# Attention's seven banks shared by maxima and scores by a fixed table, with double reads of maxima and a reordered front

## The chip, the cores and the metric

The kernel runs on one core of one Trainium2 chip. Measured is the device time of one execution in microseconds; before the change it is 4558.4 us (median of three, 4558.05 to 4560.63). PE is TensorE, ACT is ScalarE, DVE is VectorE, POOL is GpSimd, SP is SyncE.

## What is computed

Two transformer layers over 4096 tokens of width 256. Each layer adds an attention and a feed-forward branch, both read from the same normalised x.

```python
x = L0_attn_x                                   # (1, 4096, 256)
xn = _layernorm(x)
x = x + _L0_attn_ref(xn, ...) + _L0_ffn_ref(xn, ...)   # block-local linear attention; fp6-quantised linear
xn = _layernorm(x)
x = x + _L1_attn_ref(xn, ...) + _L1_ffn_ref(xn, ...)   # 16-head softmax attention; shared + 8 experts, top 2
# inside _L1_attn_ref: a layer norm of its own, q, k with rotary tables, head width 16
scores = jnp.einsum('bhqd,bhkd->bhqk', q, k)
attn = jax.nn.softmax(scores, axis=-1)
out = jnp.einsum('bhqk,bhkd->bhqd', attn, v)
```

## The kernel before, in words

The program has four phases, each with a program for every engine, ordered by semaphores alone: `front` (layer 0 and the inputs of layer 1), `attention` (layer 1's softmax attention, and on POOL the scatter of rows to the experts), `routed_experts`, and a tail.

**front** goes over 8 blocks of 512 tokens in 11 rounds. Four stages run in a round, each on another block: p (normalise, transpose, project to q, k, v; quantise), a (features of the linear attention, its windows, sums and division, the quantised linear), b (the two layer norms of layer 1, their transposes, the gate) and d (layer 1's q, k, v, the rotation, the split into three bf16 parts). PSUM holds four banks F for features, two banks W for the windows, sums and the output of a, and two banks G for all transposes and projections of p, b and d. On PE a round is: features 0 and projections d, features 1 and projections d, features 2 and values d, features 3, transposes of XD and XN (`turned`, L569, both into G), windows (L588), p's projections (L617, L623), sums (L603), transposes of XN1 and Z, the gate (L693), the outputs (L703, L708). DVE makes the products QP (L467), `turn` (L511, L512), the masks (L473), the moments, `quantise` (L416 to L428) and `divide` (L480, L481). POOL adds or subtracts for the rotation (L298), computes reciprocal roots, adds the bias to X2 (L319) and computes the lower bf16 parts (L326, L329).

**attention** has 4 groups of 4 heads and 8 blocks of 512 queries, 32 blocks n in all. A block has 128 chunks c, one for each of 32 key tiles u and 4 heads. For a chunk PE computes scores^T (128 keys x 512 queries, L1022), ACT takes the exponential into a ring of 12 (L1103), and PE weights the values with it (`weigh`, L1036: four heads side by side, columns of 32). The softmax's shift must be known before: for the block after next and the next one, PE computes 64 pairs of maxima products (`max_pair`, L1010: two heads side by side, 64 rows each), and DVE reduces each product of 512 to its maximum (L1185). At the end of a block's pairs DVE reduces them to 16 shifts (L1213), POOL splits these in two bf16 (L889 to L891), PE transposes them (L1016), DVE copies them out (L1200) and SP stores them as rows of QS (L965), so that the score products subtract them. Each block ends on ACT with a copy of the result (L1114), and ACT's program is a loop over blocks.

PE's order for round u, written out by hand: pair 2u, weighting of u-1, pair 2u+1, four scores of u+1. That is four changes of the kind of tile (64 rows, 32 columns, 64 rows, full). PSUM: four banks ST for scores, taken in turn; three banks MP for maxima, taken in turn; one bank OT for the result. A maxima product waits until its bank's last reduction is done (`room`: `mp_free`, counted per reduction). Before the first block there is a head: 64 pairs of block 0, its shifts, 12 pairs (`LEAD`) of block 1.

At the start of attention DVE computes the routing of tokens to experts in a chain of small steps (L1126 to L1178), among them the slots of the rows (L1173), after which POOL scatters. POOL first sets constant rows of KS and QS with eight memsets (L903, L904). SP issues the loads of two groups (L933, L940, L946) and only behind them the first store of shifts (L965).

Of the kernel before, what the change touches and what calls it, by code (L numbers as in the profile page):

```python
# [103 lines left out]
def front(nc, io, scr, LG):  # L104


    with ExitStack() as ctx:
        def sb(name, shape, dt=f32):
# [6 lines left out]
                 "wq_ready bias_ok store_t store_p store_v store_r store_x store_z spare")  # L115
# [150 lines left out]
        def _(pool):  # L266
# [26 lines left out]
            for it in range(ROUNDS):  # L293
                p, a, b, d = blocks(it)
                if d is not None:
                    for m in range(4):
                        pool.wait_ge(S["c_drain"], d * NC + m // 2 * 2 + 2)
                        G_.tensor_tensor(rc[:, m, :], rc[:, m, :], rs[:, m, :],  # L298
                                         ALU.add if m % 2 else ALU.subtract).then_inc(S["rot_ready"], 1)
# [13 lines left out]
                if a is not None:  # L313
                    if it == 1:
                        pool.wait_ge(S["w_load"], 16 * LOADS_W)
                        G_.tensor_tensor(bias0[:, 0, :], bias0[:, 0, :], bias0[:, 1, :], ALU.add).then_inc(S["bias_ok"], 1)
                        pool.wait_ge(S["bias_ok"], 1)
                    pool.wait_ge(S["x2_load"], 16 * (a + 1))
                    G_.tensor_tensor(X2[:], X2[:], bias0[:, 0, :].unsqueeze(1).to_broadcast([P, TPB, D]),  # L319
                                     ALU.add).then_inc(S["xb_ready"], 1)  # L320
                if d is not None:
# [5 lines left out]
                    for m in range(4):  # L327
                        pool.wait_ge(S["mid_ready"], d * 4 + m + 1)
                        G_.tensor_tensor(parts[:, 2, m, :], rc[:, m, :], parts[:, 1, m, :], ALU.subtract).then_inc(S["lo_ready"], 1)  # L329
                if p is not None and p + 1 < NB:  # L330
                    incoming(p + 1)

        @block.scalar
        def _(act):
# [10 lines left out]
            for it in range(ROUNDS):  # L345
                p, a, b, d = blocks(it)
                if a is not None:
                    for g in range(4):
                        features(a, g)
                    for k in range(DC):  # L350
                        act.wait_ge(S["x_fill"], a * NX + k + 1)
                        A.copy(xdT[:, k, :], G[:, k, :]).then_inc(S["x_drain"], 1)
                if p is not None:
                    for k in range(DC):
                        act.wait_ge(S["p_fill"], p * NP_ + k + 1)
                        A.copy(xnT[:, k, :], G[:, k, :]).then_inc(S["p_drain"], 1)
                if d is not None:
                    at_least(act, S["store_p"], d * 96)
                    for m in range(4):
                        act.wait_ge(S["rot_ready"], d * 4 + m + 1)  # L360
                        A.copy(parts[:, 0, m, :], rc[:, m, :]).then_inc(S["hi_ready"], 1)
                if b is not None:
# [8 lines left out]
                if p is not None:  # L371
                    for m in range(2 * DC):
                        act.wait_ge(S["p_fill"], p * NP_ + DC + m + 1)
                        A.copy(qkT[:, m, :], G[:, m % 2, :]).then_inc(S["p_drain"], 1)
                    for u in range(2):
                        act.wait_ge(S["p_fill"], p * NP_ + 3 * DC + u + 1)
                        A.copy(v0[:, p % 2, 2 * u:2 * u + 2, :].rearrange("p t c -> p (t c)"),
                               G[:, u, :]).then_inc(S["p_drain"], 1)
# [6 lines left out]
                if d is not None:  # L385
                    for m in range(4):
                        act.wait_ge(S["r1_ready"], d * 4 + m + 1)
                        A.copy(parts[:, 1, m, :], rc[:, m, :]).then_inc(S["mid_ready"], 1)
                if b is not None:
# [6 lines left out]
                    for k in range(DC):  # L396
# [9 lines left out]
        def _(dve):  # L406
# [96 lines left out]
            def turn(d, m):  # L503
                dve.wait_ge(S["c_fill"], d * NC + m + 1)
                if m == 0:
# [5 lines left out]
                V.scalar_tensor_tensor(to[:, 2 * n, :], bank, bqk[:, m:m + 1], tab[:, odd, :], ALU.add, ALU.mult)  # L511
# [13 lines left out]
            for it in range(ROUNDS):  # L525
# [7 lines left out]
                for g in range(4):  # L533
# [3 lines left out]
                    if d is not None and g < 2:  # L537
                        turn(d, 2 * g)
                        turn(d, 2 * g + 1)
                    if d is not None and g == 2:  # L540
                        values(d, 0)
                        values(d, 1)
                if b is not None:
                    outgoing_moments(b)
                if a is not None:
                    for h in range(H0):
                        mask(a, h)
                if p is not None:
# [15 lines left out]
        def _(pe):  # L564
# [7 lines left out]
            def features(a, g):  # L572
# [9 lines left out]
                last.then_inc(S["f_fill"], 4)  # L582

# [45 lines left out]
            for it in range(ROUNDS):  # L629
# [13 lines left out]
                if a is not None:  # L643
                    features(a, 1)
                if d is not None:
# [10 lines left out]
                if a is not None:  # L656
                    features(a, 3)
                    pe.wait_ge(S["xd_ready"], a + 1)
                    turned(free, XD, "x_fill")
                    free = ("x_drain", a * NX)  # L660
                if p is not None:
                    pe.wait_ge(S["xn_ready"], (p + 1) * TPB)
                    turned(free, XN, "p_fill")
                if a is not None:
# [1061 lines left out]
```

## Time and profile before

| | us |
|---|---|
| median of the runs | 4558.4 |
| profiled execution, its own time | 4568.3 |
| its span | 4566.5 |

Busy over the span: PE 92%, DVE 73%, ACT 58%, POOL 9%. The clock granted to PE is 0.96 of full speed in the mean, 0.87 in the front, 0.50 in the head of attention and 1.00 in its blocks. The groups of instructions name the costliest: DVE's 4096 reductions of maxima (686 ns each), ACT's 4096 exponentials (605 ns), PE's weightings, scores and maxima. Two engines are busy for over nine tenths in attention, so how long a round takes, and who waits in it, has to be read from the order of single instructions (the timeline). In a timeline row the first number is the start, the second the time until the last instruction of the row ends; x2 is the number of instructions; idle time before them stands in brackets.

### The profile page before, as it was taken

The page shows a single profiled execution, that of the slowest core. Times are in us where ns is not written, and L with a number is a line of the kernel's source. Part 1 is how long each engine was busy: PE and PEld are TensorE (multiplying, and loading weights), DVE is VectorE, ACT ScalarE, POOL GpSimd, SP SyncE. Part 2 cuts the span into 40 slices and gives each one's busy share as a digit, 9 for nine tenths or more (in the row PEclk, how much of TensorE's full clock was granted, in tenths as well). Part 3 has the DMA queues.
Part 4 walks back from the last instruction along what each step waited for, and adds up shares of the span by engine and source line. Part 5 has one row for each costly group of instructions (what it writes and reads, how often), then busy time and mean ns, then how long its engine had stood idle before and what let it go on. Part 6 is the DMA issues. An engine that isn't in the chain of part 4 may idle for free. (4 is left out here: it accounts for less than half of the span.)

```text
span 4566.5 us, 69687 instructions
## 1 busy us (share of the span) xinstructions
PE 4187.5 (92%) x23454; PEld 1823.3 (40%) x23748; DVE 3338.7 (73%) x5188; ACT 2661.5 (58%) x5113; POOL 426.7 (9%) x476
## 2 busy tenths in 40 slices
PE   6888715999999999999999999999998899999999
PEld 3665501222222222222222222222224788886666
DVE  6878578999999999999999999999980011132332
ACT  4445301777777777777777777777786222222222
POOL 0333465000000000000000000000000100011110
PEclk8989856999999999999999999999999999999999
DMA  4232384000002200002200000000003855532221
GB/s 145 75 97 74 106 146 138 4 4 6 4 4 33 50 4 6 4 4 34 50 4 6 4 4 6 4 4 6 4 6 103 248 193 193 193 122 58 63 69 42
DMA packets 206159, 264.59 MB, mean 58 GB/s; under 512 B 24881, under 2 KB 169521, under 8 KB 204241
## 3 DMA queue, kind: packets, MB, share of 16 engines
q1 hardware_dynamic: 193872, 228.98, 17.3%
q0 software_dynamic: 11904, 31.10, 2.4%
q8 instruction: 169, 2.77, 0.3%
q14 instruction: 214, 1.75, 0.1%
HBM read 184.76 MB, written 74.97 MB: 57 GB/s over the span
## 5 line engine op out<-in xcount | busy, mean ns | idle before, releaser
L1185 DVE TENSOR_REDUCE a_MX<-a_MP 128x1 f32<-128x512 f32 x4096 | 2635.9, 686 | 108.8 <-PE a_MP L1010 64.8
L1103 ACT ACTIVATE a_PT<-a_ST 128x512 f32<-128x512 f32 x4096 | 2108.0, 605 | 770.7 <-PE a_ST L1022 462.4
L1036 PE MATMUL a_OT<-a_PT,a_VG 128*32 128x512 f32 x8192 | 1092.8, 605 | 0.8 <-ACT a_PT L1103 0.5
L1022 PE MATMUL a_ST<-a_QS,a_KS 128*128 128x512 bf16 x3802 | 1036.2, 383 | 59.7 <-ACT a_PT L1103 24.5
L1010 PE MATMUL a_MP<-a_KS,a_QS 64*128 64x512 bf16 x4096 | 816.3, 395 | 129.6 <-DVE a_MX L1185 67.2
L1010 PEld LDWEIGHTS a_MP<-a_KS,a_QS 64*128 64x128 bf16 x4096 | 197.0, 93 | 1399.1 <-DVE a_MX L1185 1324.5
L1022 PEld LDWEIGHTS a_ST<-a_QS,a_KS 128*128 128x128 bf16 x4096 | 319.6, 98 | 554.4 <-ACT a_PT L1103 305.9
L1371 ACT ACTIVATE e_hT<-e_up,e_BF 128x256 f32<-128x256 f32 x312 | 147.9, 474 | 414.8 <-PE e_up L1324 414.7
L1324 PE MATMUL e_up<-e_xT,e_WF 128*128 128x256 f32 x1248 | 324.7, 383 | 0.8 <-DVE e_xT L1381 0.8
L1333 PE MATMUL e_dn<-e_WP,e_hT 128*128 128x256 f32 x1248 | 321.9, 381 | 0.0
L1381 DVE COPY e_xT<-e_tp 128x512 f32<-128x512 f32 x39 | 27.0, 692 | 364.8 <-PE e_tp L1317 364.8
L1036 PEld LDWEIGHTS a_OT<-a_PT,a_VG 128*32 128x32 f32 x8192 | 161.2, 108 | 235.4 <-ACT a_PT L1103 217.1
L1333 PEld LDWEIGHTS e_dn<-e_WP,e_hT 128*128 128x128 f32 x1248 | 238.1, 191 | 33.3
L1324 PEld LDWEIGHTS e_up<-e_xT,e_WF 128*128 128x128 f32 x1248 | 237.2, 193 | 32.5 <-DVE e_xT L1381 1.2
L889 POOL CAST a_negparts<-a_neg 128x16 bf16<-128x16 f32 x31 | 6.1, 196 | 2597.7 <-DVE a_neg L1213 2597.7
L1388 DVE TENSOR_TENSOR e_Y<-e_dn,e_BP 128x256 f32<-128x256 f32 x78 | 32.0, 424 | 233.7 <-PE e_dn L1333 233.5
L1634 ACT ACTIVATE u_hT<-u_a,t_bfs 128x512 f32<-128x512 f32 x64 | 44.0, 687 | 194.4 <-PE u_a L1589 163.2
L342 ACT ACTIVATE f_E<-f_F 128x512 f32<-128x512 f32 x128 | 79.8, 623 | 128.1 <-PE f_F L581 128.1
L1634 ACT ACTIVATE u_hT<-u_a,t_b1c 128x512 f32<-128x512 f32 x64 | 44.0, 687 | 176.4 <-PE u_a L1589 176.4
L1471 DVE RECIPROCAL t_DEN<-t_DEN 128x512 f32<-128x512 f32 x16 | 53.6, 3348 | 116.6 <-DMA t_xT<-scr_xn1T 116.6
L467 DVE SCALAR_TENSOR_TENSOR f_QP<-f_E,f_R 128x512 f32<-128x512 f32 x128 | 102.1, 826 | 37.4 <-ACT f_R L343 36.8
L1599 PE MATMUL u_d<-t_wps,u_hT 128*128 128x256 f32 x512 | 120.9, 379 | 0.0
(219 smaller groups left out, 2810.0 us busy)
## 6 DMA issues: line engine op xcount, KB each, us to landing
e_WF<-Wfc SPq DMA_DIRECT2D x39, 1024.0 KB, 5.0
e_WP<-Wproj SPq DMA_DIRECT2D x39, 1024.0 KB, 7.1
a_QS<-scr_qparts SPq DMA_DIRECT2D x384, 32.0 KB, 7.3
a_KS<-scr_kparts SPq DMA_DIRECT2D x48, 256.0 KB, 12.5
scr_xs<-f_zero SPq DMA_DIRECT2D x1, 9984.0 KB, 33.0
e_XS<-scr_xs SPq DMA_DIRECT2D x39, 256.0 KB, 2.7
scr_ys<-e_Y SPq DMA_DIRECT2D x39, 256.0 KB, 2.1
f_X<-x SPq DMA_DIRECT2D x16, 512.0 KB, 4.7
```

The lines of the kernel that those rows point to most:

```text
L342: A.activation(E[:, u % ER, :], F[:, j, :], ACT.Exp)
L467: V.scalar_tensor_tensor(QP[:, g // 2 * 4 + j, g % 2, :], E[:, u % ER, :], 1.0, R[:, u % ER, :], ALU.min, ALU.add).then_inc(S["feat"], 1)
L1010: T.matmul(bank(e + side), QS[j][half, bass.ds((b * HG + hs) * BLK + t * P, P)], KS[j][half, hs, kb * BLK:(kb + 1) * BLK], start=True, sto ...
L1022: T.matmul(ST[:, c % SBANKS, :], KS[j][:, h, u * P:(u + 1) * P], QS[j][:, bass.ds((b * HG + h) * BLK, BLK)], start=True, stop=True).then_i ...
L1036: last = T.matmul(OT[w, :], VG[j][:, u, w], PT[:, (HG * u + h) % RING, :], start=u == 0, stop=u == KT - 1)
L1103: nc.scalar.activation(PT[:, c % RING, :], ST[:, c % SBANKS, :], ACT.Exp, scale=SOFT_SCALE).then_inc(S["exp_done"], 1)
L1185: last = V.reduce_max(MX[n % 2][:, side, x:x + 1], bank(e + side), AX.X).then_inc(S["mp_free"], 1)
L1324: last = T.matmul(UP[:, m % UPB, 0:ET], WF[j][:, k, m * P:(m + 1) * P], xT[j][:, k, :], start=k == 0, stop=k == DC - 1)
L1333: last = T.matmul(DN[:, t, 0:D], hT[j][:, m, t * P:(t + 1) * P], WP[j][:, m, :], start=m == 0, stop=m == HC - 1)
L1371: nc.scalar.activation(hT[j][:, m, :], UP[:, m % UPB, 0:ET], ACT.Gelu_apprx_tanh, bias=BF[j][:, m:m + 1]).then_inc(S["hid_ready"], 1)
L1599: last = T.matmul(DN[:, t // 2, t % 2 * D:(t % 2 + 1) * D], hT[:, u % HR, t * P:(t + 1) * P], down_w[half][:, m, :], start=u == 0 and t % ...
L1634: nc.scalar.activation(hT[:, u % HR, :], A[:, use % BANKS, :], ACT.Relu if u >= HC else ACT.Gelu_apprx_tanh, bias=(tt["b1c"] if u >= HC el ...
```

## The change

In attention, the banks ST and MP become one tensor PS of seven. Which bank a chunk or a pair takes is fixed by a table with a period of eight chunks and four pairs, that is two rounds. PE's order for such a period: weighting, pairs 0 and 1, three scores, weighting, pair 2, five scores, pair 3. It has seven changes of the kind of tile. Pairs 1 and 3 are reduced by one instruction over two neighbouring banks, pairs 0 and 2 by two as before; `mp_free` now counts up by two for a double read. Waits on `ends[i]` are for the last reduction of pair i of the period. The head takes three pairs of banks in turn, all read two at once. PE's head waits for the slots, and POOL's memsets wait for them too.

In the front, XD and XN are transposed into the banks W, XD behind features 0 and XN behind features 1, and ACT's copies of them follow the same places. The rotation's additions go from POOL to DVE (`rotate`). DVE makes the masks before the moments of b. ACT copies q, k and v of p before the norms of b, and copies xn1T before the middle parts, which alternate with zT. POOL adds the bias to X2 behind the parts and after the quantising.

```diff
-SBANKS, MBANKS = 4, 3
+ABANKS = 7
+
+MAX_BANKS = ((4, 5), (0, 1), (2, 5), (2, 3))
+SCORE_BANKS = (2, 3, 6, 3, 4, 1, 0, 6)
+HEAD_BANKS = ((0, 1), (2, 3), (4, 5))
+HEAD_TURN, TURN = 6, 4
+PERIOD = len(SCORE_BANKS)
...
+        def score_bank(c):
+            return PS[:, SCORE_BANKS[(c - HG) % PERIOD], :]
...
+                event = [first_event(n)]
+
+                def pair(x):
+                    if x < PAIRS - LEAD and next1:
+                        max_pair(MAX_BANKS[x % 4], *next1, x + LEAD)
+                    elif x >= PAIRS - LEAD and next2:
+                        max_pair(MAX_BANKS[x % 4], *next2, x - PAIRS + LEAD)
+                    else:
+                        return
+                    event[0] += SIDES
+                    ends[x % 4] = event[0]
...
+                for k in range(KT // 2):
+                    c = PERIOD * k + HG
+                    at = n * CHUNKS + c
+                    if k:
+                        weigh(n, 2 * k - 1)
+                    elif n:
+                        weigh(n - 1, KT - 1)
+
+                    pe.wait_ge(S["exp_done"], at - 3)
+                    pe.wait_ge(S["mp_free"], ends[2])
+                    pair(4 * k)
+
+                    pe.wait_ge(S["exp_done"], at - 1)
+                    pair(4 * k + 1)
+
+                    pe.wait_ge(S["mp_free"], ends[3])
+                    issue(c)
+                    issue(c + 1)
+                    pe.wait_ge(S["exp_done"], at)
+                    issue(c + 2)
+                    weigh(n, 2 * k)
+
+                    pe.wait_ge(S["mp_free"], ends[0])
+                    turned = 2 * k + 1 == TURN_MAX and next1
+                    if turned:
+                        negmax_transpose(TURN, n + 1)
+                        event[0] += 1
+                        turned = event[0]
+                    pe.wait_ge(S["exp_done"], at + 1)
+                    pair(4 * k + 2)
+
+                    pe.wait_ge(S["exp_done"], at + 2)
+                    issue(c + 3)
+                    if turned:
+                        pe.wait_ge(S["mp_free"], turned)
+                    if c + HG == CHUNKS and next1:
+                        pe.wait_ge(S["negmax_load"], 16 * SIDES * (n + 2))
+                    issue(c + 4)
+
+                    pe.wait_ge(S["mp_free"], ends[1])
+                    issue(c + 5)
+                    issue(c + 6)
+                    pe.wait_ge(S["exp_done"], at + 3)
+                    issue(c + 7)
+
+                    if c + 3 < CHUNKS:
+                        pe.wait_ge(S["exp_done"], at + 4)
+                    pe.wait_ge(S["mp_free"], ends[2])
+                    pair(4 * k + 3)
...
+            def two_maxima(n, e, banks, x):
+
+                dve.wait_ge(S["mp_full"], e + SIDES)
+                V.tensor_reduce(MX[n % 2][:, :, x], PS[:, banks[0]:banks[0] + SIDES, :], AX.X,
+                                ALU.max).then_inc(S["mp_free"], SIDES)
...
+                    take = two_maxima if x % 2 else maximum
...
             pool.wait_ge(S["ident_ok"], 1)
+            pool.wait_ge(S["slots_ok"], TOPK)
             for j in range(2):
                 for side in range(SIDES):
...
+            def rotate(d, n):
+
+                dve.wait_ge(S["turned"], d * 4 + 2 * n + 2)
+                dve.wait_ge(S["c_drain"], d * NC + 2 * n + 2)
+                for m in (2 * n, 2 * n + 1):
+                    V.tensor_tensor(rc[:, m, :], rc[:, m, :], rs[:, m, :],
+                                    ALU.add if m % 2 else ALU.subtract).then_inc(S["rot_ready"], 1)
...
+                w_free = ("w_drain", b * NW + W_OUT) if b is not None else None
                 if a is not None:
                     features(a, 0)
+                    pe.wait_ge(S["xd_ready"], a + 1)
+                    turned_w(w_free, XD, "x_fill")
+                    w_free = ("x_drain", a * NX)
...
+                if p is not None:
+                    pe.wait_ge(S["xn_ready"], (p + 1) * TPB)
+                    turned_w(w_free, XN, "p_fill")
+                    w_free = ("p_drain", p * NP_)
```

## Rows read from the trace of the kernel before

**Rows 1.** Attention's full blocks: us, busy PE, PEld, DVE, ACT, POOL, PEclk, DMA, GB/s.

```profile
759.00:3422.00 2663.00, 2582.12 (x15599) 658.29 (x15885) 2549.41 (x4008) 2062.30 (x4003) 37.06 (x113) 1.00 0.06 12
```

**Rows 2.** Timeline of PE, one round: start us, us, engine line op names shapes xcount.

```profile
2055.68 0.39 PE L1010 MATMUL a_MP<-a_KS,a_QS 64*128 64x512 bf16 x2
2056.00 1.06 PE L1036 MATMUL a_OT<-a_PT,a_VG 128*32 128x512 f32 x8
2056.99 0.39 PE L1010 MATMUL a_MP<-a_KS,a_QS 64*128 64x512 bf16 x2
2057.32 1.04 PE L1022 MATMUL a_ST<-a_QS,a_KS 128*128 128x512 bf16 x3
2058.29 0.39 PE L1010 MATMUL a_MP<-a_KS,a_QS 64*128 64x512 bf16 x2
```

**Rows 3.** Timeline: DVE's reads beside PE's pairs.

```profile
2002.68 1.38 DVE L1185 TENSOR_REDUCE a_MX<-a_MP 128x1 f32<-128x512 f32 x2
2004.26 0.39 PE L1010 MATMUL a_MP<-a_KS,a_QS 64*128 64x512 bf16 x2
...
2062.29 0.39 PE L1010 MATMUL a_MP<-a_KS,a_QS 64*128 64x512 bf16 x2
2062.72 0.69 DVE L1185 TENSOR_REDUCE a_MX<-a_MP 128x1 f32<-128x512 f32 x1 [1.40 <-PE a_MP L1010]
```

**Rows 4.** Timeline of the head, where PE waits for DVE.

```profile
745.08 1.29 DVE L1185 TENSOR_REDUCE a_MX<-a_MP 128x1 f32<-128x512 f32 x2
745.82 0.10 PEld L1010 LDWEIGHTS a_MP<-a_KS,a_QS 64*128 64x128 bf16 x2 [1.29 <-issue]
```

**Rows 5.** The reduction to shifts, once a block: durations, first and last start.

```profile
L1213 DVE TENSOR_REDUCE a_neg<-a_MX x31: 286/287/289, 841.0 to 3409.1; 128x16 f32<-128x128 f32 x31
```

**Rows 6.** Timeline at a block's edge, and ACT in the last block.

```profile
2039.94 0.29 DVE L1213 TENSOR_REDUCE a_neg<-a_MX 128x16 f32<-128x128 f32 x1
...
2049.02 0.20 DVE L1200 COPY a_negT<-a_MP 32x128 bf16<-32x128 bf16 x1
...
2057.21 0.58 ACT L1114 COPY a_OS<-a_OT 128x512 f32<-128x512 f32 x1
2059.85 3.04 ACT L1103 ACTIVATE a_PT<-a_ST 128x512 f32<-128x512 f32 x6 [2.06 <-PE a_OT L1036]
...
3422.45 61.03 ACT L1103 ACTIVATE a_PT<-a_ST 128x512 f32<-128x512 f32 x124
```

**Rows 7.** DVE's reduction of 1024 elements in quantising: durations ns min/median/max, first and last start.

```profile
L416 DVE TENSOR_REDUCE f_sc<-f_XN x8: 1207/1207/1221, 9.5 to 440.6; 128x32 f32<-128x1024 f32 x8
```

**Rows 8.** Timeline before attention's first score.

```profile
603.49 6.77 DVE L1152 COPY a_PT<-a_PT 128x16 f32<-128x16 f32 x1
...
644.93 0.17 DVE L1158 TENSOR_SCALAR a_PT<-a_PT 128x8 f32<-128x8 f32 x1
...
652.76 1.29 DVE L1185 TENSOR_REDUCE a_MX<-a_MP 128x1 f32<-128x512 f32 x2 [0.82 <-PE a_MP L1010]
...
709.05 0.43 SPq L946 DMA_DIRECT2D a_VG<-scr_va  x1
...
758.88 0.13 PEld L1022 LDWEIGHTS a_ST<-a_QS,a_KS 128*128 128x128 bf16 x2 [0.44 <-issue]
```

**Rows 9.** Timeline of one round of the front, and POOL in its last.

```profile
338.94 3.40 PE L708 MATMUL f_W<-f_wout,f_attT 128*128 128x256 f32 x15
...
362.49 1.16 PE L569 MATMUL f_G<-f_ident,f_XD 128*128 128x128 f32 x8 [1.77 <-DVE f_va L519]
365.44 1.94 PE L569 MATMUL f_G<-f_ident,f_XN 128*128 128x128 f32 x8 [1.78 <-ACT f_xdT L352]
...
393.61 1.06 PE L569 MATMUL f_G<-f_ident,f_Z 128*128 128x128 f32 x8 [3.14 <-ACT f_xn1T L393]
...
403.11 3.62 PE L708 MATMUL f_W<-f_wout,f_attT 128*128 128x256 f32 x16
...
569.40 2.50 POOL L298 TENSOR_TENSOR f_rc<-f_rc,f_rs 128x512 f32<-128x512 f32 x2 [0.99 <-DVE f_rs L512]
```

More of the change, by code:

```diff
@@ L346, in _ @@
                 p, a, b, d = blocks(it)
-                if a is not None:
-                    for g in range(4):
+                for g in range(4):
+                    if a is not None:
                         features(a, g)
[L350 to L356, printed above, removed]
+                    if a is not None and g == 0:
+                        for k in range(DC):
+                            act.wait_ge(S["x_fill"], a * NX + k + 1)
+                            A.copy(xdT[:, k, :], W[:, k, :]).then_inc(S["x_drain"], 1)
+                    if p is not None and g == 1:
+                        for k in range(DC):
+                            act.wait_ge(S["p_fill"], p * NP_ + k + 1)
+                            A.copy(xnT[:, k, :], W[:, k, :]).then_inc(S["p_drain"], 1)
                 if d is not None:
@@ L361, in _ @@
                         A.copy(parts[:, 0, m, :], rc[:, m, :]).then_inc(S["hi_ready"], 1)
+                if p is not None:
+                    for m in range(2 * DC):
+                        act.wait_ge(S["p_fill"], p * NP_ + DC + m + 1)
+                        A.copy(qkT[:, m, :], G[:, m % 2, :]).then_inc(S["p_drain"], 1)
+                    for u in range(2):
+                        act.wait_ge(S["p_fill"], p * NP_ + 3 * DC + u + 1)
+                        A.copy(v0[:, p % 2, 2 * u:2 * u + 2, :].rearrange("p t c -> p (t c)"),
+                               G[:, u, :]).then_inc(S["p_drain"], 1)
                 if b is not None:
@@ L395, in _ @@
                         act.wait_ge(S["w_load"], 16 * LOADS_W)
-                    for k in range(DC):
+                for m in range(4):
+                    if d is not None:
+                        act.wait_ge(S["r1_ready"], d * 4 + m + 1)
+                        A.copy(parts[:, 1, m, :], rc[:, m, :]).then_inc(S["mid_ready"], 1)
+                    if b is not None and m % 2:
+                        k = m // 2
                         act.wait_ge(S["b_fill"], b * NB_ + DC + k + 1)
@@ L582, in features, with turned_w @@
                 last.then_inc(S["f_fill"], 4)
+            def turned_w(free, src, fill):
+                for k in range(DC):
+                    if free:
+                        at_least(pe, S[free[0]], free[1] + k + 1)
+                    transposes(W[:, k, :], src, k).then_inc(S[fill], 1)
             def windows(a, h):
@@ L657, in _ @@
                     features(a, 3)
[L658 to L664, printed above, removed]
+                    pe.wait_ge(S[w_free[0]], w_free[1] + DC)
                     for h in range(H0):
@@ L998, in _, with max_pair @@
             T = nc.tensor
-            def room(e):
-                pe.wait_ge(S["mp_free"], e + 1)
-            def max_pair(e, j, b, x):
+            ends = [HEAD_EVENTS] * len(MAX_BANKS)
+            def max_pair(banks, j, b, x):
                 h, t, kb = x // (TPB * KB), x // KB % TPB, x % KB
-                room(e + SIDES - 1)
                 for side in range(SIDES):
                     hs, half = side * HS + h, slice(side * HALF, (side + 1) * HALF)
-                    T.matmul(bank(e + side), QS[j][half, bass.ds((b * HG + hs) * BLK + t * P, P)],
+                    T.matmul(PS[:, banks[side], :], QS[j][half, bass.ds((b * HG + hs) * BLK + t * P, P)],
@@ L1011, in max_pair @@
                              KS[j][half, hs, kb * BLK:(kb + 1) * BLK], start=True, stop=True).then_inc(S["mp_full"], 1)
-            def negmax_transpose(e, n):
-                room(e)
-                wait_alone(pe, S["negmax_ready"], n + 1, S["spare"])
-                T.transpose(negT_ps(e), negparts[:].rearrange("p s r c -> p (s r c)"), identb[:]).then_inc(S["mp_full"], 1)
-            def scores(n, j, b, u):
-                for c in range(HG * u, HG * (u + 1)):
-                    pe.wait_ge(S["exp_done"], n * CHUNKS + c + 1)
-                    h = c % HG
-                    T.matmul(ST[:, c % SBANKS, :], KS[j][:, h, u * P:(u + 1) * P],
-                             QS[j][:, bass.ds((b * HG + h) * BLK, BLK)], start=True, stop=True).then_inc(S["qk_done"], 1)
@@ L1029, in weigh, with score @@
+            def score(n, j, b, c):
+                h, u = c % HG, c // HG
+                T.matmul(score_bank(c), KS[j][:, h, u * P:(u + 1) * P],
+                         QS[j][:, bass.ds((b * HG + h) * BLK, BLK)], start=True, stop=True).then_inc(S["qk_done"], 1)
             def weigh(n, u):
                 j = n // NB % 2
-                pe.wait_ge(S["exp_done"], n * CHUNKS + HG * (u + 1) + SBANKS)
+                pe.wait_ge(S["exp_done"], n * CHUNKS + HG * (u + 1))
                 if u == 0:
@@ L1075, in _ @@
             for x in range(LEAD):
-                max_pair(SIDES * (PAIRS + x) + 1, 0, 1, x)
-            scores_first(0, 0, 0)
+                head_pair(PAIRS + x, SIDES * (PAIRS + x) + 1, 0, 1, x)
+            pe.wait_ge(S["mp_free"], HEAD_EVENTS)
+            pe.wait_ge(S["negmax_load"], 16 * SIDES)
+            for c in range(HG):
+                score(0, 0, 0, c)
             for G in range(NG):
@@ L1114, in one_block @@
                 nc.scalar.copy(OS[:], OT[:]).then_inc(S["o_copied"], 1)
-            for c in range(SBANKS):
+            for c in range(HG):
                 exp(0, c)
```

156 lines of the change are left out of this document (62 added, 94 removed).

## The prediction

> **What bounds the kernel now.** I read the busy time by stretch first: the front ends at 588, attention's first scores come at 759, its full blocks end at 3422 and the last block at 3486; the experts and the tail behind it aren't touched. In the full blocks PE is busy for 2582 of 2663 us (97%) and VectorE for 2549 (96%) [rows 1], so the groups of instructions can't say which of them sets the pace. The timeline can [rows 2]. One round of PE starts a maxima pair at 2055.68, the weighting at 2056.00, a pair at 2056.99, four scores at 2057.32 and the next pair at 2058.29: 0.32 + 0.99 + 0.33 + 0.97 = 2.61 us, the same in round after round. A score takes 0.22 and a pair alone the same; what is over, about 0.10, comes at each of the four changes of tile kind. VectorE's two reads of a pair together span 1.29, one alone 0.69 [rows 3], so the second begins 0.61 after the first: four reads need 2.43 of the 2.61. Nor does PE wait for them: in the head, where it does, its weights start 0.05 after a read ends (745.08 + 0.69 = 745.77, then 745.82) [rows 4], but in the round the read of 2002.68 + 0.69 = 2003.37 to 2004.06 is followed by a pair only at 2004.26 [rows 3]. **PE's order of work is the bound**, VectorE comes 7% behind it.
>
> A block lasts (3409.1 - 841.0)/30 = 85.60 us [rows 5]; 32 rounds are 83.5, and 2.1 are left: VectorE idles for 1.40 behind ScalarE's block loop (copy at 2057.21, next exponential only at 2059.85), and the transposition of the maxima with its copy and the wait for it make the rest [rows 3, 6].
>
> **Attention, the steady round.** Two rounds are now one period: weighting, pairs P0 and P1, three scores, weighting, P2, five scores, P3. There are seven changes for eight, all on PE, so by PE alone the period is 2 x 2.61 - 0.10 = **5.12 us** for 5.22. P1 and P3 are read two banks at once. No row shows that read from PSUM; the nearest is the 1024-element reduction in SBUF, 1207 ns beside the 0.69 of a PSUM read of 512 [rows 3, 7]: 512 more elements for 0.52. So I take 1.21, with the next read 1.13 after its start. VectorE then needs 4 x 0.61 + 2 x 1.13 = 4.70 of 5.12, which looks like room.
>
> The bank table takes it away. P3 is issued only when mp_free has reached ends[2], that is when both reads of P2 are done, and VectorE reads in order P0 (two single reads), P1 (one double), P2 (two single). From P0's start: 0.43 until the first read (2062.29 to 2062.72) [rows 3], 0.61, 0.61, then the double for 1.13, then 0.61 and 0.68 to the end of P2: 4.07. Release 0.05, so P3 starts at 4.12. Where would PE be? P0 and P1 0.22 + 0.32, three scores 0.66 + 0.10, weighting 0.99, P2 0.32, five scores 1.08 + 0.10: 3.79. It waits 0.33. After P3 come 0.32 and a weighting of 1.00 before the next P0, and VectorE has nothing to read in that time but P3: free again at 0.43 + 1.13 = 1.56 behind P3's start, while P0's products are there at 1.32 + 0.43 = 1.75. The cycle closes over both engines: 4.12 + 1.32 = **5.44 us per two rounds, 0.22 more than now**. The other new waits hold: P1's read frees its banks at 0.43 + 1.22 + 1.21 + 0.05 = 2.91 for a score (the third behind P2) due at about 3.05; P3's frees its own 0.15 before the first score of the next period; and the exponential of the score behind P2, for which P3 waits too, is done at 2.62 + 0.5 + 0.6 = 3.7, 0.4 ahead of P3 (a product ends 0.39 after its start [rows 2], six exponentials take 3.04, some 0.6 for one and 0.48 from one to the next [rows 6]). Ends for the unknown double: it would have to cost 0.33 less than 1.13 for PE to be the bound again; that is 0.80 for 1024 elements, and the SBUF row excludes it unless PSUM reads two banks faster than one. A cost above is possible: 0.1 more would be 1.6 us a block.
>
> The rule against which I weighed the gain is in the Trainium skill, "TensorEngine Tiling (Array Packing)", Key Properties: changing the tiling mode drains TensorE. The trace agrees: the 0.10 at each change. By that rule alone the period would be 5.12.
>
> **The block's edge.** ScalarE's copy and loop jump (2.64 from the copy's start to the exponential [rows 6], for 0.5 without them) delay the first exponential of the next block's second score group by 1.8 against the schedule; P2 needs its bank, so P2 moves by 1.2 and P3 by 1.1 (now 1.4). The copy of the transposed maxima (0.20 plus its own wait) stands in VectorE's queue before P2, which is in the cycle: 0.3. The small reduction before P0 (0.29 [rows 6]) takes the reads some 0.2 later, and there is room for 0.05: 0.15. Together 1.5 for 2.1. A block: 16 x 5.44 + 1.5 = 88.6, **+3.0; 31 blocks: +93 us**. With 0.05 of doubt in the cycle this is 70 to 120.
>
> **The last block** has no pairs and is bound by exponentials: 61.0 us for 124 [rows 6]. The new order makes a score wait for a weighting twice in eight (0.2 and 0.35 late): 16 x 0.45 = **+7 us** (0 to 12).
>
> **The head.** Before, GpSimd's eight memsets (6.9 each) run beside VectorE's routing steps, and from 603.49 on each small copy or scalar step there lasts until a memset ends: 41 us until 644.93 for ten instructions that take some 2.3 undisturbed [rows 8]. The memsets now wait for the slots, so these 39 us go. The slots are ready at about 611; the first loads have been issued from 588.6 on at 0.5 each and land, at 12.5 us for one of the keys' (the page), at about the same time. The moved memsets can hold the last two small steps instead (up to 2 x 6.9), so the maxima begin at 612 to 626; I take 625. 64 pairs take 64 x 1.13 = 72 (now 76 pairs and the shifts fill 652.76 to 758.88, 1.4 a pair [rows 8]), then 2, then 12 x 1.13: 713. But SyncE stores the negated maxima only behind both groups' loads, whose last is issued at 709.05 [rows 8] and, as the page has it, needs 10.2 us: the first score comes at about 720 for 758.88: **-38 us** (-30 to -48). GpSimd's scatter starts some 16 later and ends by 806 for 790; the first block's shifts are wanted at about 805, so it just hides.
>
> The shared port behind this is also in the Trainium skill, "SBUF - State Buffer", SBUF: two separate sides: VectorE in a two-port mode and GpSimd lock each other out for a whole instruction. The trace agrees, 6.8 us each.
>
> **The front.** A round lasts 64.2 us (the weighting by w_out at 338.94 and 403.11). In it PE idles 1.77 before the XD transposes, 1.78 before XN, and 3.14 before Z [rows 9], and 2.8 in three smaller gaps. The transposes move into banks W between features, so the first two gaps go, but the masks wait for the last features on ScalarE, which stay: windows end some 3 earlier. Splitting ScalarE's copies (xn1T ahead of the middle parts) takes 2 of the 3.14, while XN1 and Z behind the value copies give back 1. The rotation leaves GpSimd for four VectorE steps of about 0.65 (a VectorE step of 512 elements, [rows 3], is the nearest row); VectorE's products beside it ran slower by as much, so that is even. I get 3.7 a round for seven rounds and 3.4 at the end, where the rotation on GpSimd stands in the last chain (2.50 for two of its four steps [rows 9]): **-30 us** (-10 to -50). The moved bias addition waits for X2, reloaded 12 later; it ends about 2 before it is needed. If that cover goes, 2 us a round go too.
>
> **Sum.** -30 - 38 + 93 + 7 = +32 on the profile's 4568.3 us (span 4566.5), so 4600 there; the median of the runs is 4558.4, 9.9 lower, so **4590 us**.
>
> **Rivals.** (1) PE sets the period after all: if VectorE's chain from P0 to P2's end is under 3.74, P3 doesn't wait. That is 5.12, 5.1 us a block less than in my sum: 4590 - 159 = 4431. For it speaks the total of 4.70 for VectorE, against it the chain above. 0.10. (2) The steady loss is right, but front and head give all they can (-50, -48) and the cycle is 5.40: -20 - 10 - 20 = 4540. 0.08. (3) The loads, the scatter or the bias addition eat half of the gain in front and head: 4590 + 34 = 4624; together with a double read of 1.2 spacing 4660. 0.14. The forecast itself has 0.68, with a range of 4560 to 4620.
>
> 0.2% is 9 us, about what a measurement of this kernel can tell from no change. Under 4549: (1), most of (2): 0.16. Within: 0.06. Above: 0.78. The range takes in (2) and half of (3): 4540 to 4640.
>
> **What the profile will show.** Pairs P3 of successive periods 5.44 apart, PE's weights of P3 idle behind VectorE by some 0.3, none elsewhere; double reads of 1.21; 88.6 between two small reductions; first score near 720; front's end near 558. Wrong would be: a double read far from 1.21, a change from scores straight to the weighting that costs much more than 0.10 and over the slack of 0.33, or GpSimd's scatter late for the first block.

## The result and the profile after

The changed kernel takes 4626.5 us (median of four runs, 4624.3 to 4627.5) where the kernel before takes 4559.2 beside it: 1.0147 times as long, 95% interval 1.0129 to 1.0164. Forecast were 4590, slower, within 4540 to 4640. The sign and the waiting pair held; the loss is 67 us where the sum gave 32. The profiled execution of after took 4626.0 (span 4624.2), 57.7 more than the one of before, so the two profiles show 58 of the 67 us; the other 9 are the size of a stall that the profile of before has in its first block (before_again, below).

The page of after, its busy times and the costliest groups. A read of two banks takes 1221 ns, one of a single bank 684:

```profile
PE 4179.7 (90%) x23748; PEld 1784.1 (39%) x23748; DVE 3141.6 (68%) x4158; ACT 2666.9 (58%) x5113; POOL 374.8 (8%) x444
...
L1253 DVE TENSOR_REDUCE a_MX<-a_PS 128x2 f32<-128x1024 f32 x1062 | 1290.4, 1221 | 326.6 <-PE a_PS L1031 326.5
L1259 DVE TENSOR_REDUCE a_MX<-a_PS 128x1 f32<-128x512 f32 x1972 | 1266.3, 684 | 48.7 <-PE a_PS L1031 42.2
...
L1031 PE MATMUL a_PS<-a_KS,a_QS 64*128 64x512 bf16 x4096 | 730.7, 391 | 261.0 <-ACT a_PT L1172 160.3
```

VectorE has lost 197 us of work (3338.7 before) and the kernel is slower: VectorE's load was not what set the pace. PE idles 261 us ahead of the maxima pairs, where it idled 130. Busy time by stage of after (front; head; blocks; last block), in the columns of [rows 1]. The blocks have PE at 2573 of 2781 us, where it was at 2582 of 2663 [rows 1]:

```profile
0.00:553.00 553.00, 442.61 (x2948) 313.23 (x2948) 394.86 (x627) 265.94 (x515) 135.69 (x155) 0.90 0.33 108
553.00:679.00 126.00, 48.09 (x159) 9.26 (x160) 116.77 (x138) 0.42 (x1) 74.67 (x33) 0.50 0.93 165
679.00:3460.00 2781.00, 2572.76 (x15812) 625.95 (x15811) 2402.56 (x3019) 2058.61 (x3978) 68.76 (x144) 1.00 0.06 13
3460.00:3543.00 83.00, 73.86 (x445) 17.44 (x443) 0.21 (x1) 76.57 (x149) 0.58 (x3) 1.00 0.01 4
```

The reduction to shifts, once a block, the counterpart of [rows 5]. The 30 blocks between the first and the last take (3459.6 - 752.9)/30 = 90.2 us each, for 85.6:

```profile
L1289 DVE TENSOR_REDUCE a_neg<-a_MX x31: 285/286/288, 752.9 to 3459.6; 128x16 f32<-128x128 f32 x31
```

Stage by stage, in us from the timelines (first attention load, first score, first and last such reduction, last score, end of the span):

| | front | to the first score | to the first reduction | 30 blocks | to the last score | rest |
|---|---|---|---|---|---|---|
| before | 587.7 | 171.2 | 82.1 | 2568.1 | 72.5 | 1084.9 |
| after | 553.0 | 125.6 | 74.3 | 2706.7 | 82.8 | 1081.8 |
| difference | -34.7 | -45.6 | -7.8 | +138.6 | +10.3 | -3.1 |

One period of after, of all engines. Read it by P0 (2002.78), P2 (2005.06) and P3 (2006.96):

```profile
2002.78 0.61 PE L1031 MATMUL a_PS<-a_KS,a_QS 64*128 64x512 bf16 x4
2003.20 1.29 DVE L1259 TENSOR_REDUCE a_MX<-a_PS 128x1 f32<-128x512 f32 x2
...
2004.41 1.22 DVE L1253 TENSOR_REDUCE a_MX<-a_PS 128x2 f32<-128x1024 f32 x1
2005.06 0.39 PE L1031 MATMUL a_PS<-a_KS,a_QS 64*128 64x512 bf16 x2
2005.38 1.25 PE L1046 MATMUL a_PS<-a_QS,a_KS 128*128 128x512 bf16 x5
2005.54 1.28 DVE L1259 TENSOR_REDUCE a_MX<-a_PS 128x1 f32<-128x512 f32 x2
2006.93 0.12 PEld L1031 LDWEIGHTS a_PS<-a_KS,a_QS 64*128 64x128 bf16 x2 [0.79 <-ACT a_PT L1172]
2006.96 0.39 PE L1031 MATMUL a_PS<-a_KS,a_QS 64*128 64x512 bf16 x2 [0.32 <-ACT a_PT L1172]
2007.28 1.06 PE L1056 MATMUL a_OT<-a_PT,a_VG 128*32 128x512 f32 x8
2008.28 0.39 PE L1031 MATMUL a_PS<-a_KS,a_QS 64*128 64x512 bf16 x2
```

The period is 8.28 - 2.78 = 5.50 us; its median over the blocks is 5.506, for 5.220 before. The chain is the forecast's: 0.42 to the first read, two single reads in 1.21, the double for 1.13, two single reads for 1.28, and only then P3; 0.32 and 1.00 more to the next P0. Between the last read's end (2005.54 + 1.28 = 2006.82) and P3's product (2006.96) lie 0.14.

### The profile page after: what moved, and what is told of

Read it like the earlier page. It is cut to its first block and busy times, and to the rows that moved or that the text cites. A ratio compares the mean times of both kernels' runs of the same rounds, so it can differ in the third digit from the quotient of the medians.

```text
span 4624.2 us, 71502 instructions
## 1 busy us (share of the span) xinstructions
PE 4179.7 (90%) x23748; PEld 1784.1 (39%) x23748; DVE 3141.6 (68%) x4158; ACT 2666.9 (58%) x5113; POOL 374.8 (8%) x444
## 5 line engine op out<-in xcount | busy, mean ns | idle before, releaser
L1172 ACT ACTIVATE a_PT<-a_PS 128x512 f32<-128x512 f32 x4096 | 2117.7, 603 | 852.3 <-PE a_PS L1046 787.7
L1253 DVE TENSOR_REDUCE a_MX<-a_PS 128x2 f32<-128x1024 f32 x1062 | 1290.4, 1221 | 326.6 <-PE a_PS L1031 326.5
L1259 DVE TENSOR_REDUCE a_MX<-a_PS 128x1 f32<-128x512 f32 x1972 | 1266.3, 684 | 48.7 <-PE a_PS L1031 42.2
L1046 PE MATMUL a_PS<-a_QS,a_KS 128*128 128x512 bf16 x4096 | 1071.4, 382 | 14.6 <-ACT a_PT L1172 8.8
L1031 PE MATMUL a_PS<-a_KS,a_QS 64*128 64x512 bf16 x4096 | 730.7, 391 | 261.0 <-ACT a_PT L1172 160.3
L1031 PEld LDWEIGHTS a_PS<-a_KS,a_QS 64*128 64x128 bf16 x4096 | 173.7, 94 | 1343.5 <-ACT a_PT L1172 816.3
L1046 PEld LDWEIGHTS a_PS<-a_QS,a_KS 128*128 128x128 bf16 x4096 | 313.7, 97 | 625.7 <-DVE a_MX L1253 296.6
```

The costliest lines, as they stand in the source:

```text
L1031: T.matmul(PS[:, banks[side], :], QS[j][half, bass.ds((b * HG + hs) * BLK + t * P, P)], KS[j][half, hs, kb * BLK:(kb + 1) * BLK], start=Tr ...
L1046: T.matmul(score_bank(c), KS[j][:, h, u * P:(u + 1) * P], QS[j][:, bass.ds((b * HG + h) * BLK, BLK)], start=True, stop=True).then_inc(S["q ...
L1172: nc.scalar.activation(PT[:, c % RING, :], score_bank(c), ACT.Exp, scale=SOFT_SCALE).then_inc(S["exp_done"], 1)
L1253: V.tensor_reduce(MX[n % 2][:, :, x], PS[:, banks[0]:banks[0] + SIDES, :], AX.X, ALU.max).then_inc(S["mp_free"], SIDES)
L1259: V.reduce_max(MX[n % 2][:, side, x:x + 1], PS[:, banks[side], :], AX.X).then_inc(S["mp_free"], 1)
```

## The experiments

The theory: a block's period runs through VectorE, because P3 waits until both reads of P2 are done. The rivals: the double reads as such cost more than they save; the loss comes from somewhere else in the new order (the changes of tile kind, ScalarE's waits); front and head change the blocks too. Of before, the median beside these runs was 4568.6 (first four) and 4574.5 us (last four), so ratios are what to compare; stages compare directly, and where a ratio and the stages differ the text goes by the stages.

**before_again.** The kernel before once more, unchanged, to see how its stages vary.

> The kernel before, unchanged, for a second profile: its profiled execution took 4568 us where its median is 4559, and the profile of the changed kernel (4626 us) lies on its median. If the 9 us are chance of one execution, this profile shows about 4559 us; then the difference sits in one stretch, most likely the front or the loads ahead of attention (DMA), while the blocks of attention stay at 85.6 us.

4566.4 us, where 4559 was expected. Head 171.0, blocks 85.5 us each and last block 72.5 are as in the profile of before. Two stretches differ: the front takes 595.5 for 587.7, and from the first score to the first reduction are 72.7 for 82.1. The 9.4 there are a stall. Two windows of before, then the counterpart in before_again, in the columns of [rows 1]:

```profile
770.00:790.00 20.00, 12.98 (x78) 3.19 (x78) 12.42 (x21) 10.70 (x21) 12.26 (x13) 0.95 0.34 111
788.00:795.00 7.00, 4.87 (x18) 0.94 (x18) 3.87 (x6) 2.63 (x5) 0.96 (x1) 0.51 0.11 38
```

```profile
777.00:797.00 20.00, 20.00 (x126) 5.01 (x118) 19.73 (x32) 15.64 (x31) 11.33 (x12) 1.00 0.31 106
```

PE comes out of the head at 0.50 of its clock (the head's window of after, above) and gets the full one 8.8 us behind the first score in both profiles, at 767.7 and at 775.4. Then PE idles for 7.0 of 20 us in before and not at all in before_again. The longest gap, 2.89, ends at 790.13. PE waits there for a read before which VectorE had idled for 2.99, though its product was there at 786.24. Within that gap, at 788.1, the clock falls back to 0.50 until 795.0. What held VectorE the profile doesn't show. So the -7.8 of the table is this one execution's: beside the 72.7 of before_again (and 72.6 in front_only) the 74.3 of after are 1.6 more. The front's own end varies by 8 us.

**front_only.** Does the front hold its part, and does it touch anything behind it? The front is that of after, attention that of before; of the edit the hunks of the diff shown ahead:

```diff
+            def rotate(d, n):
...
                 if a is not None:
                     features(a, 0)
+                    pe.wait_ge(S["xd_ready"], a + 1)
+                    turned_w(w_free, XD, "x_fill")
...
-                if d is not None:
-                    for m in range(4):
-                        pool.wait_ge(S["c_drain"], d * NC + m // 2 * 2 + 2)
-                        G_.tensor_tensor(rc[:, m, :], rc[:, m, :], rs[:, m, :],
```

> The kernel before with the changed front alone. The front of the changed kernel ends 34.7 us earlier (553.0 for 587.7). If that is all its own and nothing later depends on it: 4559 - 35 = 4524 us. If part of it was chance of the profiled execution: 4530 to 4535. If an earlier end only makes the loads of attention start in more traffic: over 4540.

4521.0 us, 0.9904 of before (0.9887 to 0.9921). The front ends at 554.1; from there to the first score 171.1, blocks of 85.54, a period of 5.220. The front is a gain of 34 to 41 us by its end, and head and blocks stay as they were. The span is 46 to 48 us shorter than those of the two profiles of before: the stall's 9.4 beside the first, and 3 to 5 behind attention, where the other runs vary by 4.

**p3_first.** P2 takes the banks (2, 5) and is read in that order, bank 2 first. P3 takes (2, 3). The wait asks for both reads; the banks need only the first:

```diff
                     if c + 3 < CHUNKS:
                         pe.wait_ge(S["exp_done"], at + 4)
-                    pe.wait_ge(S["mp_free"], ends[2])
+                    pe.wait_ge(S["mp_free"], ends[2] - 1)
                     pair(4 * k + 3)
```

> The changed kernel, but the fourth pair of a period waits for the first of the two reads of the third pair (its bank 2), not for both; bank 5 is still waited for ahead of the next period's first pair. Theory: the cycle over VectorE's five reads sets the period of 5.51 us. With the wait 0.61 shorter the fourth pair starts when TensorE gets there or the exponential of the fourth score is done, the period falls to 5.12 to 5.2, a block from 90.0 to 84 to 85.2, and the time to 4430 to 4470 us. Rival: the loss is in the kinds of tile or the exponentials, and this wait hides it only: then the period stays over 5.4 and the time over 4590 us.

4438.1 us, **0.9719 of before (0.9701 to 0.9737)**, where after is at 1.0147: some 190 us less by one number. The period is 5.113. Its timeline, the counterpart of the one above:

```profile
2002.25 0.61 PE L1031 MATMUL a_PS<-a_KS,a_QS 64*128 64x512 bf16 x4
2002.68 1.29 DVE L1259 TENSOR_REDUCE a_MX<-a_PS 128x1 f32<-128x512 f32 x2
...
2004.54 0.39 PE L1031 MATMUL a_PS<-a_KS,a_QS 64*128 64x512 bf16 x2
2004.86 1.25 PE L1046 MATMUL a_PS<-a_QS,a_KS 128*128 128x512 bf16 x5
2005.02 1.27 DVE L1259 TENSOR_REDUCE a_MX<-a_PS 128x1 f32<-128x512 f32 x2
2006.05 0.39 PE L1031 MATMUL a_PS<-a_KS,a_QS 64*128 64x512 bf16 x2
...
2007.37 0.61 PE L1031 MATMUL a_PS<-a_KS,a_QS 64*128 64x512 bf16 x4
```

P3 now starts at 2006.05, while the second read of P2 runs until 2006.29. It comes 3.80 after P0 (the forecast had 3.79 for PE by itself), and the next P0 at 5.12. Everything up to P3 stands at the same distances as in after; all of the loss of the blocks is this one wait. With it gone PE is the bound at seven changes of tile kind, 0.107 less than at eight (5.220 to 5.113). That the 0.107 is the missing change is read from the count; no run varies it alone. The tile kinds and ScalarE are not the cause of the loss.

**all_single.** Are the double reads the loss? In the blocks each is made two single ones, the order and the waits stay:

```diff
-                    take = two_maxima if x % 2 else maximum
+                    take = maximum
```

> The changed kernel with every pair of the blocks read bank by bank (the head keeps its double reads). Theory: the read of the second pair is in the cycle that sets the period, and two single reads take 2 x 0.61 = 1.22 from start to start where the double takes 1.13: the period grows by 0.09 to 5.60, a block by 1.4, the time by 40 to 48 us to about 4670. Rival: double reads are themselves what slows VectorE (a read across two banks is held up by TensorE's writes); then single reads are as fast or faster, 4600 to 4626 us.

4655.7 us, 1.0194 of before (1.0174 to 1.0213), period 5.567. VectorE's chain from P0 to the end of P2 holds one double; made single it costs 2 x 0.61 for 1.13, so 0.09, and 0.061 was measured. The rival falls: double reads are worth 0.06 a period in this order.

**p3_first_single.** The same with P3's wait mended: `take = maximum` in p3_first.

> The mended kernel (fourth pair waits for the first read of the third pair) with all pairs of the blocks read bank by bank. Theory: with that wait mended TensorE's order sets the period (5.113), VectorE needs 8 x 0.61 = 4.88 of it and its cycle has room, so reading two banks at once brings nothing in the blocks: the period stays at 5.11 to 5.13, the time within 12 us of p3_first (4438). Rival: VectorE is near enough that waits show: a period of 5.2 and 4465 us.

4439.5 us, 0.9711 (0.9697 to 0.9724), period 5.113 as in p3_first. Once PE is the bound, six reads or eight make no difference in the blocks.

**swap_waits.** The release of 0.14 where the head showed 0.05 [rows 4]. P3 has two waits, on ScalarE's exponentials and on VectorE's reads. They are exchanged, nothing else:

```diff
+                    pe.wait_ge(S["mp_free"], ends[2])
                     if c + 3 < CHUNKS:
                         pe.wait_ge(S["exp_done"], at + 4)
-                    pe.wait_ge(S["mp_free"], ends[2])
                     pair(4 * k + 3)
```

> The changed kernel with the two waits ahead of the fourth pair written in the other order (reads first, then exponentials), nothing else. In the changed kernel's trace the wait for the reads stands as an instruction of its own before the pair's weights, since the weights carry the one for the exponentials, and the product starts 0.14 us after the read's end, where the forecast had 0.05. Theory: 0.06 to 0.09 of this is the separate wait; carried by the weights themselves, the period falls from 5.51 to about 5.44, a block by 1.0 to 1.3, the time by 30 to 40 us to about 4590. Rival: the 0.14 is what a change of tile kind costs after an idle stretch; then nothing moves (within 5 us of 4626).

4582.3 us, 1.0024 of before (1.0015 to 1.0033); the span is 43 us shorter than that of after, by the order of two waits. (The ratios are 56 us apart; the 30 blocks together take (90.22 - 88.72) x 30 = 45 less, which bears out the span.) The period is 5.413, 0.093 less. Its timeline at P2's reads and P3:

```profile
2004.29 1.28 DVE L1259 TENSOR_REDUCE a_MX<-a_PS 128x1 f32<-128x512 f32 x2
2005.62 0.10 PEld L1031 LDWEIGHTS a_PS<-a_KS,a_QS 64*128 64x128 bf16 x2 [0.86 <-DVE a_MX L1259]
2005.62 0.39 PE L1031 MATMUL a_PS<-a_KS,a_QS 64*128 64x512 bf16 x2 [0.37 <-DVE a_MX L1259]
```

From the read's end, 2005.57, to P3 are 0.05, as in the head; in the median of the blocks it is 0.058, where after has 0.146. The releaser that the profile names for the weights changes with it. The waits of PE's weight loads between 1000 and 3300 us (us in total, times, longest), first after, then swap_waits:

```profile
PEld a_PS L1031 <- ACT a_PT L1172: 678.7, 844, 0.9
PEld a_PS L1031 <- DVE a_MX L1259: 299.4, 357, 0.8
```

```profile
PEld a_PS L1031 <- DVE a_MX L1259: 608.6, 779, 0.9
PEld a_PS L1031 <- ACT a_PT L1172: 359.2, 442, 0.8
```

One of the two waits stands in the trace as an instruction of its own. It has line 1127, the wait that is written second: in after the one for VectorE's reads, in swap_waits the one for the exponentials. Around the P3 shown, first after, then swap_waits:

```profile
L1127 PEldq EVENT_SEMAPHORE  x1: 51/51/51, 2006.9 to 2006.9; - x1
L1127 PEldq EVENT_SEMAPHORE  x1: 51/51/51, 2005.0 to 2005.0; - x1
```

In after it comes only behind the read's end (2006.82), and the weights follow it at 2006.93. In swap_waits it is done 0.5 before the read ends, and the weights wait for the read by themselves. So the weights carry the wait written first, and the other stands before them; when that one ends last, 0.06 more go by until the weights start and 0.09 until the product does. The Trainium skill, "Perfetto Trace Analysis", Identifying Dependency Chains, describes such instructions: one that waits for several engines may get separate semaphore instructions ahead of it. The trace agrees, with the rows above.

**memsets_early.** GpSimd's wait for the slots goes back behind the eight memsets, all else as in after:

```diff
-            pool.wait_ge(S["slots_ok"], TOPK)
             for j in range(2):
...
             pool.wait_ge(S["ones_ok"], 4 * SIDES)
+            pool.wait_ge(S["slots_ok"], TOPK)
```

> The changed kernel with the eight memsets where they were, beside VectorE's routing steps. Theory: ten small steps are stretched again to a memset each, so the maxima of the head start at 64 us behind the front's end, not at 36 (the two stretched steps of the changed kernel fall away, 13 us), and 64 + 12 double reads at 1.13 bring the first score to 553 + 64 + 73 + 2 + 14 = 706 for 678.6: +27; the scatter starts some 35 earlier and its 6 us in the second block go: in all +20, about 4647. If the first score is bound by the group loads instead, it stays near 680 and the time near 4620.

4651.7 us, 1.0171 (1.0154 to 1.0188). Front to first score takes 152.5 for 125.6 (128.4 to 129.0 in the four other runs with this head), so moving the memsets gives 24 to 27 of the head's 46 us. The remaining 19 (171.2 to 152.5) belong to the rest of the head's edits, which I didn't take apart. VectorE's small steps are held again, each until a memset ends, as in [rows 8]; the last held one and the first free one:

```profile
606.43 6.85 DVE L1226 TENSOR_SCALAR a_PT<-a_PT 128x8 f32<-128x8 f32 x1
613.32 0.17 DVE L1227 TENSOR_SCALAR a_PT<-a_PT 128x8 f32<-128x8 f32 x1
```

On the other side the first interval between two reductions is 89.9 here and 96.3 in after: the scatter, later in after, costs 6.4.

**both_mended.** A version for use: p3_first, with the constant rows of the second pair of KS and QS set only after the first shifts (so the scatter starts four memsets earlier), and with scores of the last block taking all seven banks in turn, four a round as before:

```diff
+        def last_bank(c):
+            return PS[:, (2, 3, 5, 4, 1, 0, 6)[(c - HG) % 7], :]
...
+            constant_rows(0)
+            pool.wait_ge(S["ones_ok"], 2 * SIDES)
...
+                if n == 1:
+                    pool.wait_ge(S["negmax_ready"], 2)
+                    constant_rows(1)
```

> The mended kernel with two more losses taken away. (1) The last block has the old order of scores and weightings and its exponentials a ring of seven banks: the last 72.5 us from the last reduction to the last score as before, where the changed kernel has 82.8: -10. (2) Only group 0's constant rows are set ahead of the scatter, group 1's behind the first shifts: the scatter starts 28 us earlier, the shifts of the second block no longer wait for it, and the stretch between the first two reductions in the blocks falls from 96.4 to about 84: -12. Together 4438 - 22 = 4416 us. Rival to (2): the late step there is the loads, not the scatter; then that stretch stays at 96. Rival to (1): exponentials are bound by something else in the last block; then 82.8 stays.

4427.0 us, **0.9681 of before (0.9666 to 0.9695)**, the fastest of all. The last block takes 73.0 for 82.8 and the first interval 83.6 for 96.4, as expected; but front to first score takes 133.6 for 128.5, and 4416 us had been expected in all. The first score's row in both_mended, with SP's last load and the store of the shifts ahead of it:

```profile
677.06 0.44 SPq L978 DMA_DIRECT2D a_VG<-scr_va  x1
677.60 6.25 SPq L997 DMA_DIRECT2D a_QS<-a_negT  x2
...
689.89 1.49 PE L1056 MATMUL a_PS<-a_QS,a_KS 128*128 128x512 bf16 x3 [12.07 <-DMA a_QS<-a_negT]
```

By the first score the scatter has 33 stores and 5 loads beside the first loads (16 and 3 in p3_first), SP's last load goes out 4 us later behind the front's end, and the store takes 12 us to release PE, where it took 10.6. That this traffic is the cause is argued, not tried by itself. Of the 23 us of the two places 5 are given back so; the spans of p3_first and both_mended are 18.5 apart, their medians, taken beside different runs of before, 11.

## Why the forecast was right in sign and short by half

**The bound of before: right.** PE's order of work set the pace: 197 us less for VectorE brought nothing, p3_first_single beside p3_first shows it at no cost, and one change of tile kind less brought 0.107 in two rounds. The rule of the Trainium skill, "TensorEngine Tiling (Array Packing)", Key Properties, that a change of mode drains TensorE, is in agreement with it, as far as the count shows; by that rule alone the period would be 5.12, and 5.113 is what p3_first shows.

**The period: mechanism right, the release mis-sized.** Forecast 4.12 + 1.32 = 5.44, measured 5.506. All reads fit (double 1.22 for 1.21). The step that failed is the term "Release 0.05": it was taken from the head, where one wait was in play; P3 has two, and the late one, standing as an instruction of its own, cost 0.14. swap_waits gives the forecast's 5.44 within 0.03 (5.413). Price: 0.066 x 16 x 30 = +32 us on the 30 blocks.

**"The bank table takes it away": wrong as a reason.** The table would allow P3 after the first read of P2. What took the gain was the count in the wait, one more than the table needs. I had the slack of PE (0.33) worked out and never asked which of the two reads P3's banks depend on.

**The block's edge: 1.5 forecast, 89.96 - 16 x 5.506 = 1.86 measured**, +11 us on 30 blocks. P2 is held there by ScalarE's loop jump, as forecast. The edge of after; in the steady rounds P2 comes 2.28 after P0, here 3.62, so 1.34 late for a forecast of 1.2:

```profile
2036.38 0.61 PE L1031 MATMUL a_PS<-a_KS,a_QS 64*128 64x512 bf16 x4
...
2039.25 4.12 ACT L1172 ACTIVATE a_PT<-a_PS 128x512 f32<-128x512 f32 x8 [2.07 <-PE a_OT L1056]
2040.00 0.39 PE L1031 MATMUL a_PS<-a_KS,a_QS 64*128 64x512 bf16 x2 [1.26 <-ACT a_PT L1172]
...
2043.16 0.60 PE L1031 MATMUL a_PS<-a_KS,a_QS 64*128 64x512 bf16 x4
```

P0 to P0 is 6.78 for 5.50 here, 1.28 (forecast 1.1); the other 0.6, by subtraction, are the small reduction and the copy of the transposed maxima (forecast 0.45).

**The scatter "just hides": wrong**, +6 us. GpSimd computes the first block's shifts only at 763.84, though the reduction came at 752.93; the transposition waits, and PE idles 4.14 before it:

```profile
752.93 0.29 DVE L1289 TENSOR_REDUCE a_neg<-a_MX 128x16 f32<-128x128 f32 x1
...
763.84 0.20 POOL L913 CAST a_negparts<-a_neg 128x16 bf16<-128x16 f32 x1 [1.55 <-issue]
...
764.70 0.27 PE L1042 MATMUL a_PS<-a_identb,a_negparts 128*32 128x128 bf16 x1 [4.14 <-issue]
```

I had the scatter's end and the shifts' due time 1 us apart. On this clock (34.7 less) that was the first score at 685, the shifts due at 770, the scatter's end at 771. They came at 679, 753 and 763: the shifts were due 17 earlier, the scatter was done only 8 earlier. And the wait costs more than its 4.14: within it PE's clock falls to half, until 770.3 (the columns of [rows 1]):

```profile
763.51:770.33 6.82, 5.63 (x20) 1.22 (x22) 2.72 (x4) 2.57 (x5) 0.61 (x3) 0.50 0.01 4
```

In memsets_early the clock stays full there and the interval is 89.9; in p3_first PE idles for 10.65 in this place, the clock is at half from 764.1 to 777.8, and the first interval is 12.8 longer than the later ones. Named as cover, the scatter should have carried a price.

**The last block: +7 forecast, +10.3 measured.** ScalarE waits twice in eight exponentials, as here in after:

```profile
3500.77 1.57 ACT L1172 ACTIVATE a_PT<-a_PS 128x512 f32<-128x512 f32 x3 [0.18 <-PE a_PS L1046]
...
3505.25 1.09 ACT L1172 ACTIVATE a_PT<-a_PS 128x512 f32<-128x512 f32 x2 [0.18 <-PE a_PS L1046]
```

Eight take 3505.25 - 3500.77 = 4.48, where without gaps they take 61.03/124 x 8 = 3.94 [rows 6]: 0.54 a period for the 0.45 forecast, 16 times; the other 1.7 us I didn't trace. both_mended, with four scores a round again and seven banks in turn, takes the same block in 73.0, so the new order together with its table is the cause; no run parts the two.

**The head: -38 forecast, -42 to -46 measured.** The maxima begin 36 after the front's end, where 37 were forecast, and the last two small steps are held by two memsets, as forecast. The two-bank read, from PSUM, is not: three in 3.49 us beside a memset of 6.92:

```profile
576.40 6.03 DVE L1246 TENSOR_SCALAR a_PT<-a_PT 128x39 f32<-128x39 f32 x1
...
582.46 6.87 DVE L1247 CAST g_owner<-a_PT 128x39 uint32<-128x39 f32 x1
589.34 6.92 POOL L928 MEMSET a_KS<- 32x8192 bf16 x1
589.41 3.49 DVE L1253 TENSOR_REDUCE a_MX<-a_PS 128x2 f32<-128x1024 f32 x3
```

Then SP's loads decide, as forecast: the last is issued at 667.71, the shifts' store behind it at 668.25, the first score starts at 678.61. That load had been put at 709.05 - 34.7 = 674.4 on this clock; that it left 7 earlier is the miss, and I didn't test why.

**The front: -30 forecast, -35 measured.** From one weighting by w_out to the next (317.10 to 376.74) a round lasts 59.6 for 64.2, so 4.5 a round were won for the 3.7 counted. The 3.14 before Z have become 1.45, and the gaps before XD and XN are gone. A gap of 3.49 is there instead within the windows, behind the fourth, where PE waits for VectorE's masks to free a bank:

```profile
344.68 8.53 PE L603 MATMUL f_W<-f_QP 128*128 128x128 f32 x48 [3.49 <-DVE f_SW L472]
...
369.64 1.07 PE L577 MATMUL f_G<-f_ident,f_Z 128*128 128x128 f32 x8 [1.45 <-ACT f_xn1T L387]
```

**The sum of the misses**, on the profiled executions: blocks +48.6 (32 period, 11 edge, 6 scatter), last block +3.3, front -4.7, head -7.6, first block -10.8 (-9.4 of it the stall of before's profile; beside before_again it took 1.6 more, for +3), rest -3.1: +25.7, which is 4626.0 for a forecast of 4600.3. Then I had taken 9.9 off, because the profile of before lay that much over its median, about what its stall cost; that of after lay at its median. This is the other part of the 36.5 by which 4590 was too low. The rivals: (1), PE as the bound, 4431, is p3_first but for 7 us, so the price was right, the condition not met. (2) and (3) had the front and the head off in either direction; they came out a little better than forecast and were outweighed.

## What to carry to other kernels

Where buffers are shared by a table, write down for each wait which read of which buffer it really needs; here one count too many in a wait on a two-step release turned a gain of 128 us into a loss of 67. Of two waits ahead of an instruction, try writing the one that ends last first: in the one place tried it cost nothing and was worth 0.09 us a period. In a forecast, take a release's price from a place with the same number of waits, and give every "it just hides" a price of its own.

## What the runs showed of the hardware beyond that

A wait that ends last costs 0.14 or 0.05 us from the releasing read's end to the next product, by its place among two waits (after, swap_waits). A VectorE reduction over two neighbouring PSUM banks takes 1221 ns, 147 less than two over one (2 x 684); behind one another the gain is less, 1.13 from one start to the next for 2 x 0.61. It goes on unhindered beside a GpSimd memset that holds small SBUF steps for 6.0 to 6.9 us. A long gap of PE in the first block brought a stretch at half clock with it, which adds to its price: the clock fell within the gap of 4.14 in after (0.50 from 763.5 to 770.3) and within the one of 2.89 in before (0.50 from 788.1 to 795.0).
